# One queue for all first inputs of a two-layer adaLN, FFN and expert kernel, in a new order, and ones from a set tile

## The chip, the cores and the metric

The kernel runs on one core of one Trainium2 chip. The metric is the device time in microseconds of one execution, as the median over runs. The core has five engines that run their own instruction lists: TensorE (PE, with its weight loads shown apart as PEld), VectorE (DVE), ScalarE (ACT), GpSimd (POOL) and SyncE (SP). Transfers between memory and the on-chip buffer are issued from SP's queue and ScalarE's queue (and GpSimd's, for indirect ones) and are carried by 16 DMA engines. Engines wait for each other and for transfers on semaphores.

## The reference

The input x is 32 x 32 x 512 numbers; each of the two layers adds the output of a feed-forward block to x, and each block works on a conditioned version of x.

```python
# layer 0
c0 = conv1d(x, L0_cond_weight, groups=4, taps=9, pad=4) + (cond @ c_weight.T)[:, :, None] + bias
g, u = octonion_linear(c0, ternary(w_gate)), octonion_linear(c0, ternary(w_up))   # 512 -> 1360
x = x + octonion_linear(silu(g) * u, ternary(w_down))                            # 1360 -> 512
# layer 1
h = gelu(cond @ W0 + b0); h = gelu(h @ W1 + b1); att = softmax(h @ W2 + b2)       # 32 x 8
y = mix of 8 channel kernels by att, applied to x, plus att @ bias_k
out = x + top-2-of-32 experts of y (512 x 512 each, routed per token)
```

`ternary(W)` is scale * clip(round(W / scale), -1, 1) with scale = mean(|W|) over the whole table, so nothing of a table can be quantized before all of it has been read and summed.

## The kernel before

All is written by hand as one instruction list per engine, with semaphores; the order of each list is the order of the code. What matters here is the start, the first 16 of 280 us. The small arrays lie in host-packed groups: `nets` (condition, the small nets' weights, biases, a row of constants) is one array of 281 KB, `cf` (identity matrix, counters, masks, a block of ones) one of 187.5 KB, `mix` holds the sign patterns `perm` in its first half.

The steps of the start, by engine, with lines of the kernel before:

- SP (L566 to L580) issues without waiting: `base[0]` (gate table, 352 KB), `perm` (256 KB), `wc` (taps, 192 KB), `xp_first` (half of the padded input, 1040 KB), `base[1]` and `base[2]` (up and down tables), `sel`, the rest of `mix`, `xp_second`, `kept`, `eb`, `x` into `acc`, and two fills of memory tables.
- ScalarE (L753, L754) issues `nets` and `cf` as its first two instructions.
- VectorE sets `fill` and `unit` (L919, L920, a 128 x 128 tile of ones), then for table m: `magnitudes(m)` (L926, sum of |base|), `scales(m)` (L931 to L933), `quantize_first(m)` (L940, L941).
- TensorE: ten `fills` (L1398, matmuls on a constant tile whose result nobody reads), `scale(0)` (L1348: ones times the row sums), two fills, the first net layer (L1407), the context (L1409 and L1410, where `ones` times a row adds the bias), fills and second net layer, `gate_table(0)` and `(1)` (L1357), the convolution's first block (L1330), the third net layer (L1421, L1422, again with `ones`), two gate tables, `scale(1)`, the second block, two gate tables, the third block, two gate tables, and `across_conv` (L1340, transposes by the identity matrix in `cf`).

`pe.wait_ge(cf_in, 16)` stands ahead of the first net layer. VectorE waits for `cf` only after the down table's scale (after L1008), and the ternary remainder on GpSimd (L670 to L673) follows `thr_done`.

Of the kernel before, what the change touches and what calls it, by code (L numbers as in the profile page):

```python
# [42 lines left out]
P = 128  # L43
NB, CH, D = 32, 32, 512
# [13 lines left out]
KC = 8  # L58
# [160 lines left out]
def split(ap, group):  # L219

    out, at = [], 0
    for _, w in GROUPS[group]:
        out.append(ap[:, at:at + w])
        at += w
    return out


def build_adaln_ffn(nc, a):
    ctx = ExitStack()
    with ctx:  # L230
# [21 lines left out]
        def put(name, shape, dt, at):  # L252
            return nc.alloc_sbuf_tensor_at(name, shape, dt, offset=at)

        def own(name, shape, dt):
            n = 4 if dt != BF16 else 2
            for s in shape[1:]:
                n *= s
            return put(name, shape, dt, region(n))
# [41 lines left out]
        nets = su.put("nets", [P, NETS], F32)  # L301
# [3 lines left out]
        cond, cwt, w0s, w1s, w2s, b01, rows = split(nets[:], "nets")  # L305
# [3 lines left out]
        base = put("base", [P, 3, BW], F32, r_h + 2 * HC * HALF * 4 - 3 * BW * 4)  # L309
# [3 lines left out]
        unit = put("unit", [P, P], F32, r_t + 2 * D * 4 + 1024)  # L313
# [45 lines left out]
        cf = own("cf", [P, CF_W], F32)  # L359
# [39 lines left out]
        NETS_BANK, SCALE_BANK = bank[4], bank[7]  # L399
# [25 lines left out]
        def sem(name):  # L425
            return ctx.enter_context(nc.semaphore(name))

        wc_in, cf_in, nets_in, mix_in, sel_in, kept_in, eb_in = (
            sem(s) for s in ("wc_in", "cf_in", "nets_in", "mix_in", "sel_in", "kept_in", "eb_in"))
        base_in = [sem(f"base_in{m}") for m in range(3)]  # L430
# [7 lines left out]
        ctx_mm = sem("ctx_mm")  # L438
        h1_mm, h1_done, h2_mm, h2_done = (sem(s) for s in ("h1_mm", "h1_done", "h2_mm", "h2_done"))
        att_mm, att_out, att_max, att_exp, att_done = (sem(s) for s in ("att_mm", "att_out", "att_max", "att_exp", "att_done"))  # L440
# [52 lines left out]
        ones = cf[:, C_ONE:C_ONE + P]  # L493

        def rec_parts(g):

            tiles, parts_ = GROUPS_OF_TILES[g], []
            for q, (p0, w, _, pos) in enumerate(tiles[0]):
                ranks = [tile[q][2] for tile in tiles]
                runs = [0] + [i for i in range(1, len(ranks)) if ranks[i] != ranks[i - 1] + 1] + [len(ranks)]  # L500
                for i0, i1 in itertools.pairwise(runs):
                    same = [p for p in parts_ if [p[0] + p[1], p[2], p[3] + p[1], p[4:]] == [p0, ranks[i0], pos, [i0, i1]]]
                    if same:
                        same[0][1] += w
                    else:
                        parts_.append([p0, w, ranks[i0], pos, i0, i1])
            return parts_
# [9 lines left out]
        def height(t):  # L517

            return sum(w for _, w, _, _ in TILES[t])
# [44 lines left out]
        def _(sp):  # L564

            sp.dma_start(base[:, 0], a["base"][:, 0]).then_inc(base_in[0], 16)  # L566
            sp.dma_start(mix[:, 0:OCT * P // 2], a["mix"][:, 0:OCT * P // 2]).then_inc(perm_in, 16)
            sp.dma_start(wc[:], a["wc"]).then_inc(wc_in, 16)
            sp.dma_start(xp_first[:], a["xp"][:, 0:NB // 2]).then_inc(xp_in[0], 16)
            for m in range(1, 3):  # L570
                sp.dma_start(base[:, m], a["base"][:, m]).then_inc(base_in[m], 16)
            sp.dma_start(sel[:], a["sel"]).then_inc(sel_in, 16)
            sp.dma_start(mix[:, OCT * P // 2:], a["mix"][:, OCT * P // 2:]).then_inc(mix_in, 16)
            sp.dma_start(xp_second[:], a["xp"][:, NB // 2:]).then_inc(xp_in[1], 16)
# [175 lines left out]
        @block.scalar  # L750
        def _(act):

            act.dma_start(nets[:], a["nets"]).then_inc(nets_in, 16)  # L753
            act.dma_start(cf[:], a["cf"]).then_inc(cf_in, 16)  # L754

            def conv_hi(i):
                act.wait_ge(across_mm, i + 1)
# [563 lines left out]
        def _(pe):  # L1321
            mm = nc.tensor.matmul
# [13 lines left out]
            def across_conv(i):  # L1336

                pe.wait_ge(convs_done, i + 1)
                for b in range(NPT):
                    v = nc.tensor.transpose(ACROSS[FIRST_TILES[i]][:, P * b:P * (b + 1)], convs[:, i % 2, b], ident)  # L1340
                v.then_inc(across_mm, 1)
# [8 lines left out]
            def gate_table(k):  # L1350

                if k == 0:
                    pe.wait_ge(tern_done, 1)
                    pe.wait_ge(perm_in, 16)
                if k >= 2:
                    pe.wait_ge(pg_done, k - 1)
                mm(in_bank(PG[k % 2], 0, CUT), perm[:, k], chunks(0, CUT)(tern[:, 0]), start=True, stop=True).then_inc(pg_mm, 1)  # L1357

            def up_table(k):

                if k == 0:
                    pe.wait_ge(tern_done, 2)
                if k >= 2:
                    pe.wait_ge((pu_even, pu_odd)[k % 2], k // 2)
                mm(in_bank(PU[k % 2], 0, CUT), perm[:, k], chunks(0, CUT)(tern[:, 1]), start=True, stop=True).then_inc(pu_mm, 1)
# [29 lines left out]
            def fills(count):  # L1395

                for _ in range(count):
                    mm(bank[0][:], fill[:, 0:P], fill[:], start=True, stop=True)  # L1398
# [4 lines left out]
            scale(0)  # L1403
            fills(2)
            pe.wait_ge(nets_in, 16)
            pe.wait_ge(cf_in, 16)
            mm(NETS_BANK[:, 0:NB], w0s, cond, start=True, stop=True).then_inc(h1_mm, 1)  # L1407
            pe.wait_ge(thr_done, 1)
            mm(SCALE_BANK[:, 0:NB], cwt, cond, start=True, stop=False)  # L1409
            mm(SCALE_BANK[:, 0:NB], rows[0:1, 0:P], ones[0:1, 0:NB], start=False, stop=True).then_inc(ctx_mm, 1)  # L1410
            fills(1)
            pe.wait_ge(h1_done, 1)
            mm(NETS_BANK[:, NB:2 * NB], w1s, h1[:], start=True, stop=True).then_inc(h2_mm, 1)
# [5 lines left out]
            conv(0, (0,))  # L1419
            pe.wait_ge(h2_done, 1)  # L1420
            mm(NETS_BANK[0:NB, 64:64 + KC], h2[:], w2s, start=True, stop=False)  # L1421
            mm(NETS_BANK[0:NB, 64:64 + KC], ones[0:1, 0:NB], rows[0:1, P:P + KC], start=False, stop=True).then_inc(att_mm, 1)  # L1422
            gate_table(2)
            gate_table(3)
            scale(1)
# [4 lines left out]
            gate_table(6)  # L1430
            gate_table(7)
            pe.wait_ge(att_out, 1)
            across_conv(0)
            up_table(0)
            pe.wait_ge(thr_done, 2)
# [167 lines left out]
            def product(t, c0, c1):  # L1603

                if c0 == 0:
                    pe.wait_ge(xt_done, t + 1)
                    if t >= 2:
                        pe.wait_ge(res_done, t - 1)
                    if t < 2:
                        pe.wait_ge(h_done, 2 * HC)  # L1610
                    for _, _, r, _ in TILES[t]:
                        pe.wait_ge(w_in[buffer(r)], loads_of(r))
                for c in range(c0, c1):
                    for p0, w, r, _ in TILES[t]:
                        v = mm(RS[t % 2][p0:p0 + w], xT[x_slot(t)][:, c, p0:p0 + w], wbuf[buffer(r)][:, c], start=(c == 0), stop=(c == DC - 1))  # L1615
                if c1 == DC:
                    v.then_inc(r_mm, 1)
# [269 lines left out]
```

## Time and profile before

| | us |
|---|---|
| median of 3 runs | 280.45 (280.31 to 280.61) |
| profiled execution | 282.07 |
| its span | 280.2 |
| TensorE busy | 263.7 (94%) |
| VectorE busy | 143.0 (51%) |
| ScalarE busy | 77.8 (28%) |
| GpSimd busy | 68.8 (25%) |

The span runs from the first to the last recorded instruction; the execution's own time is 1.9 us longer. The shares are means over the whole span. In the first 1/40 of it TensorE's digit is 7 and DMA's 7, then DMA stands at 9 for four slices, so the start is a stretch of its own. "Idle before" in a row names what ended the wait. A landing time is the time from a transfer's issue to the semaphore that tells it is complete.

### The profile page before, as it was taken

Reading aid. Unit: us, or ns where it says so; the run is one execution under the profiler, and the core shown is the slowest. Engines: PE = TensorE matmul, PEld = TensorE weight load, DVE = VectorE, ACT = ScalarE, POOL = GpSimd, SP = SyncE. Lnnn points to the kernel's source line nnn. Section 1 sums busy time; section 2 is a strip of 40 time slices with the busy share of each in tenths; the row PEclk is TensorE's granted clock in tenths of the full one; section 3 lists DMA queues with packets and bytes.
Section 4 is the critical chain, followed back from the end, with each engine's and each line's share of the span. In section 5 each row is a group of like instructions: output and inputs, shape, how many; then the busy total and the mean of one; then the engine's idle time right before and its main releaser. Section 6 shows DMA issues by size and latency. Waiting matters only on the chain.

```text
span 280.2 us, 4479 instructions
## 1 busy us (share of the span) xinstructions
PE 263.7 (94%) x1584; PEld 157.3 (56%) x1584; DVE 143.0 (51%) x420; ACT 77.8 (28%) x144; POOL 68.8 (25%) x67
## 2 busy tenths in 40 slices
PE   7988999999999999999999999999979999998970
PEld 2456676688866678878886664423333433332750
DVE  2677765766913341577441445510558521440695
ACT  1665564334221215223321222221010101113100
POOL 0621600000000000004605023445755352133200
PEclk9999999999999999999999999999999999999996
DMA  7999900000000100019807999944899999994945
GB/s 256 399 374 328 291 18 1 2 0 2 0 37 37 40 1 37 2 25 388 338 2 251 394 425 422 418 146 113 326 321 388 414 420 421 423 378 168 413 163 223
DMA packets 19590, 61.69 MB, mean 220 GB/s; under 512 B 4698, under 2 KB 6394, under 8 KB 15216
## 3 DMA queue, kind: packets, MB, share of 16 engines
q1 hardware_dynamic: 14816, 51.03, 47.6%
q0 software_dynamic: 3312, 7.80, 7.5%
q10 hardware_dynamic: 1440, 2.58, 2.5%
q8 instruction: 13, 0.21, 0.3%
q14 instruction: 9, 0.07, 0.1%
HBM read 54.39 MB, written 13.21 MB: 241 GB/s over the span
## 4 chain that ended last, share of the span: by engine, by line
PE 75%; DVE 10%; DMA 8%; issue 2%; another core or an unknown queue 2%; SPq 1%; ACT 1%; DVEq 0%; ACTq 0%; POOLq 0%
PE bank L1447 28%; PE bank L1615 16%; PE bank L1650 15%; PE bank L1502 3%; DMA xp_first<-in_xp 3%; DVE acc L1303 3%; DMA wbuf<-r_tab 3%; PE bank L1588 2%; PE bank L1330 2%; DMA r_tab<-res,recs 2%; PE bank L1509 1%; DVE acc L1077 1%; PE bank L1340 1%; DVE xT L1109 1%
## 5 line engine op out<-in xcount | busy, mean ns | idle before, releaser
L1615 PE MATMUL bank<-wbuf,xT 128*32 128x512 f32 (+1 forms) x448 | 70.5, 598 | 1.6 <-DVE xT L1109 0.9
L1650 PE MATMUL bank<-md,hid 128*128 128x512 f32 x176 | 49.6, 418 | 0.0
L683 POOL DMA_INDIRECT slots<-kept,sid x16 | 15.9, 996 | 120.3 <-DVE sid L1072 117.3
L1615 PEld LDWEIGHTS bank<-wbuf,xT 128*32 128x32 f32 (+1 forms) x448 | 18.7, 119 | 37.7 <-issue 34.6
L1650 PEld LDWEIGHTS bank<-md,hid 128*128 128x128 f32 x176 | 31.3, 189 | 8.9 <-issue 4.1
L1447 PE MATMUL bank<-y0hi,mg 128*128 128x512 f32 x88 | 35.2, 412 | 0.2 <-ACT y0hi L758 0.2
L1447 PE MATMUL bank<-y0hi,mu 128*128 128x512 f32 x88 | 33.7, 396 | 0.7 <-DVE mu L958 0.7
L1447 PE MATMUL bank<-y0lo,mu 128*128 128x512 f32 x88 | 33.6, 393 | 0.0
L1447 PE MATMUL bank<-y0lo,mg 128*128 128x512 f32 x88 | 33.5, 392 | 0.0
L1109 DVE COPY xT<-bank 128x512 f32<-128x512 f32 x19 | 12.9, 690 | 38.5 <-PE bank L1588 32.7
L880 ACT ACTIVATE res<-bank,recs 128x512 f32<-128x512 f32 x19 | 13.1, 688 | 67.8 <-PE bank L1615 52.4
L1018 DVE TENSOR_TENSOR htmp<-bank,stmp 128x512 f32<-128x512 f32 x22 | 15.2, 690 | 28.9 <-PE bank L1447 18.4
L690 POOL DMA_INDIRECT yg<-y_tab,recs x19 | 19.4, 1021 | 18.3 <-DMA recs<-slots 13.1
L698 POOL DMA_INDIRECT r_tab<-res,recs x16 | 17.0, 1064 | 26.6 <-ACT res L880 21.9
L803 ACT ACTIVATE hid<-htmp 128x512 fp32r<-128x512 f32 x22 | 13.9, 630 | 24.4 <-DVE htmp L1018 22.4
L799 ACT ACTIVATE stmp<-bank,small 128x512 f32<-128x512 f32 x22 | 15.2, 689 | 17.9 <-PE bank L1447 17.6
L1028 DVE SCALAR_TENSOR_TENSOR acc<-bank,small,acc 128x512 f32<-128x512 f32 x8 | 6.0, 750 | 25.8 <-PE bank L1650 19.8
L1447 PEld LDWEIGHTS bank<-y0hi,mg 128*128 128x128 f32 x88 | 16.5, 188 | 4.7 <-issue 1.5
L1447 PEld LDWEIGHTS bank<-y0hi,mu 128*128 128x128 f32 x88 | 16.5, 188 | 4.7 <-ACT mu L773 1.1
L1447 PEld LDWEIGHTS bank<-y0lo,mg 128*128 128x128 f32 x88 | 16.5, 188 | 3.3 <-issue 0.2
L1447 PEld LDWEIGHTS bank<-y0lo,mu 128*128 128x128 f32 x88 | 16.4, 188 | 3.2
L1022 DVE TENSOR_TENSOR hid<-htmp,hid 128x512 fp32r<-128x512 f32 x22 | 16.0, 729 | 0.9 <-ACT hid L803 0.3
(205 smaller groups left out, 289.9 us busy)
## 6 DMA issues: line engine op xcount, KB each, us to landing
wbuf<-in_w SPq DMA_DIRECT2D x32, 1024.0 KB, 12.8
r_tab<-in_zero SPq DMA_DIRECT2D x1, 4096.0 KB, 24.7
wbuf<-r_tab SPq DMA_DIRECT2D x8, 512.0 KB, 7.7
acc<-in_x SPq DMA_DIRECT2D x1, 2048.0 KB, 14.6
y_tab<-yv SPq DMA_DIRECT2D x8, 256.0 KB
out<-acc ACTq DMA_DIRECT2D x8, 256.0 KB, 2.3
base<-in_base SPq DMA_DIRECT2D x3, 352.0 KB, 7.6
xp_first<-in_xp SPq DMA_DIRECT2D x1, 1040.0 KB, 7.5
```

Of the source, the lines that this page charges most:

```text
L683: pool.indirect_dma_start(out=slots, out_offset=bass.IndirectOffsetOnAxis(ap=sid[:, j, k:k + 1], axis=0), in_=rec[:, j, k], in_offset=None ...
L690: pool.indirect_dma_start(out=yg[b][0:rows_], out_offset=None, in_=y_tab[0:HALF] if first else y_tab, in_offset=bass.IndirectOffsetOnAxis( ...
L698: pool.indirect_dma_start(out=r_tab, out_offset=bass.IndirectOffsetOnAxis(ap=recs[0:rows_, slot, 1:2].bitcast(U32), axis=0), in_=res[b][0: ...
L799: nc.scalar.activation(stmp[:, n % 2], G[n % 2][:], ACT.Silu, scale=wsc[:, 0:1]).then_inc(silu_done, 1)
L803: nc.scalar.activation(hid[:, :, 0, n % HC], tiles_of(htmp[:, n % 2]), ACT.Copy).then_inc(hhi_done, 1)
L880: nc.scalar.activation(res[b][0:rows_], bank_[0:rows_], ACT.Copy, scale=recs[0:rows_, slot, 2:3].bitcast(F32)).then_inc(res_done, 1)
L1018: nc.vector.tensor_tensor(htmp[:, n % 2], UU[n % 2][:], stmp[:, n % 2], ALU.mult).then_inc(h_done, 1)
L1022: nc.vector.tensor_tensor(hid[:, :, 1, n % HC], tiles_of(htmp[:, n % 2]), hid[:, :, 0, n % HC].bitcast(F32), ALU.subtract).then_inc(hlo_do ...
L1109: nc.vector.tensor_copy(xT[half_][:].rearrange("p c t -> p (c t)"), bank_[:]).then_inc(xt_done, 1)
L1447: v = mm(bank_[:], tab[:, r, n % HC], (y0hi, y0lo)[part][half][:, r], start=(r == 0 and part == 0), stop=(r == R - 1 and part == 1))
L1615: v = mm(RS[t % 2][p0:p0 + w], xT[x_slot(t)][:, c, p0:p0 + w], wbuf[buffer(r)][:, c], start=(c == 0), stop=(c == DC - 1))
L1650: v = mm(DN[j % 2][:], hid[:, t, part, c], md[:, c], start=(c == 0 and part == 0), stop=(c == HC - 1 and part == 1))
```

## The change

`nets` and `cf` are issued by SP's queue and no longer by ScalarE's. On SP's queue `nets` stands second, after `base[0]`; `cf` stands between `base[1]` and `base[2]`. The two small matrix products that multiply by a row of ones read it from the tile `unit` that VectorE sets, in place of the block of ones in `cf`. TensorE's wait for `cf` moves from the first net layer to the first transposes.

```diff
             sp.dma_start(base[:, 0], a["base"][:, 0]).then_inc(base_in[0], 16)
+            sp.dma_start(nets[:], a["nets"]).then_inc(nets_in, 16)
             sp.dma_start(mix[:, 0:OCT * P // 2], a["mix"][:, 0:OCT * P // 2]).then_inc(perm_in, 16)
             sp.dma_start(wc[:], a["wc"]).then_inc(wc_in, 16)
             sp.dma_start(xp_first[:], a["xp"][:, 0:NB // 2]).then_inc(xp_in[0], 16)
-            for m in range(1, 3):
-                sp.dma_start(base[:, m], a["base"][:, m]).then_inc(base_in[m], 16)
+            sp.dma_start(base[:, 1], a["base"][:, 1]).then_inc(base_in[1], 16)
+            sp.dma_start(cf[:], a["cf"]).then_inc(cf_in, 16)
+            sp.dma_start(base[:, 2], a["base"][:, 2]).then_inc(base_in[2], 16)
...
-            act.dma_start(nets[:], a["nets"]).then_inc(nets_in, 16)
-            act.dma_start(cf[:], a["cf"]).then_inc(cf_in, 16)
...
             pe.wait_ge(nets_in, 16)
-            pe.wait_ge(cf_in, 16)
             mm(NETS_BANK[:, 0:NB], w0s, cond, start=True, stop=True).then_inc(h1_mm, 1)
...
-            mm(SCALE_BANK[:, 0:NB], rows[0:1, 0:P], ones[0:1, 0:NB], start=False, stop=True).then_inc(ctx_mm, 1)
+            mm(SCALE_BANK[:, 0:NB], rows[0:1, 0:P], unit[0:1, 0:NB], start=False, stop=True).then_inc(ctx_mm, 1)
...
-            mm(NETS_BANK[0:NB, 64:64 + KC], ones[0:1, 0:NB], rows[0:1, P:P + KC], start=False, stop=True).then_inc(att_mm, 1)
+            mm(NETS_BANK[0:NB, 64:64 + KC], unit[0:1, 0:NB], rows[0:1, P:P + KC], start=False, stop=True).then_inc(att_mm, 1)
...
             pe.wait_ge(att_out, 1)
+            pe.wait_ge(cf_in, 16)
             across_conv(0)
```

SP's queue at the start of the program, before:

```order
L566 DMA base<-in_base 128x704
L567 DMA mix<-in_mix 128x512
L568 DMA wc<-in_wc 128x384
L569 DMA xp_first<-in_xp 128x2080
L571 DMA base<-in_base 128x704 x2
L572 DMA sel<-in_sel 32x192
```

And after:

```order
L566 DMA base<-in_base 128x704
L567 DMA nets<-in_nets 128x562
L568 DMA mix<-in_mix 128x512
L569 DMA wc<-in_wc 128x384
L570 DMA xp_first<-in_xp 128x2080
L571 DMA base<-in_base 128x704
L572 DMA cf<-in_cf 128x375
L573 DMA base<-in_base 128x704
L574 DMA sel<-in_sel 32x192
```

`nets` and `cf` are two more rows on this queue, and every transfer from `perm` on is issued one place later, from `base[2]` on two. On ScalarE the same two rows are gone:

```order
-L750 UNCONDITIONAL_BRANCH [waits barrier_Pool_Activation_PE_DVE_SP_release]
-L753 DMA nets<-in_nets 128x562
-L754 DMA cf<-in_cf 128x375
+L752 UNCONDITIONAL_BRANCH [waits barrier_Pool_Activation_PE_DVE_SP_release]
 L762 ACT_TABLE_LOAD
 L762 ACTIVATE h_67<-bank,nets 128x32 [waits h1_mm]
```

ScalarE's first own work is now the table load. On TensorE no instruction changes its place; at the net layers and the transposes the waits and operands change:

```order
-L1407 MATMUL bank<-nets 128x32 [waits cf_in,nets_in]
-L1409 MATMUL bank<-nets 128x32 [waits thr_done]
-L1410 MATMUL bank<-cf,nets 128x32
+L1406 MATMUL bank<-nets 128x32 [waits nets_in]
+L1408 MATMUL bank<-nets 128x32 [waits thr_done]
+L1409 MATMUL bank<-unit,nets 128x32
```

The wait for `cf` is now part of the first transpose's row, L1340, ahead of all transposes.

## Rows read from the trace of the kernel before

**Rows 1.** Chain of waits, first 40 us: start us, us, what

```profile
2.09 7.51 DMA xp_first<-in_xp
...
11.92 1.07 PE bank L1330 x32
```

**Rows 2.** Timeline, TensorE: start, us, engine line operation [idle before]

```profile
1.43 4.45 PE L1398 MATMUL bank<-fill 128*128 128x512 bf16 x10 [1.43 <-DVE fill L919]
...
6.45 0.35 PE L1348 MATMUL bank<-asum,unit 128*128 128x1 f32 x2 [0.58 <-DVE mag L926]
...
7.70 0.40 PE L1410 MATMUL bank<-cf,nets 1*128 1x32 f32 x2
...
8.62 0.49 PE L1357 MATMUL bank<-tern,mix 128*128 128x384 bf16 x2
...
9.74 1.15 PE L1330 MATMUL bank<-xp_first,wc 32*32 32x512 f32 x32 [0.63 <-DMA xp_first<-in_xp]
...
11.54 0.38 PE L1348 MATMUL bank<-asum,unit 128*128 128x1 f32 x2
...
15.52 0.63 PE L1340 MATMUL bank<-cf,convs 128*128 128x128 f32 x4 [0.59 <-DVE convs L948]
```

**Rows 3.** Timeline, VectorE

```profile
5.41 0.89 DVE L926 SCALAR_TENSOR_TENSOR mag<-base 128x704 f32<-128x704 f32 x1 [3.89 <-DMA base<-in_base]
...
8.44 0.18 DVE L982 COPY cbt<-bank 128x32 f32<-128x32 f32 x1
10.58 0.89 DVE L926 SCALAR_TENSOR_TENSOR mag<-base 128x704 f32<-128x704 f32 x1 [1.97 <-issue]
11.40 0.08 DVE L926 DVE_READ_ACCUMULATOR mag<-base 128x1 f32 x1
```

**Rows 4.** Timeline, SP's and ScalarE's queues

```profile
0.70 0.40 SPq L566 DMA_DIRECT2D base<-in_base  x1
...
1.15 0.46 ACTq L754 DMA_DIRECT2D cf<-in_cf  x1
...
2.90 1.20 SPq L571 DMA_DIRECT2D base<-in_base  x2
```

**Rows 5.** Transfers by source: KB each, median us to landing; last, the three of base

```profile
base<-in_base SPq DMA_DIRECT2D x3, 352.0 KB, 7.6
...
nets<-in_nets ACTq DMA_DIRECT2D x1, 281.0 KB, 4.8
...
cf<-in_cf ACTq DMA_DIRECT2D x1, 187.5 KB, 5.5
...
DMA to landing us min/median/max: 4.7/7.6/7.8
```

**Rows 6.** Stretches: bounds, length, busy time of each engine, PEclk, DMA share, GB/s

```profile
2.20:3.70 1.50, 1.50 (x5) 0.60 (x4) 0.00 (x0) 0.72 (x1) 0.00 (x0) 1.00 0.76 236
...
2.20:8.00 5.80, 5.22 (x19) 2.37 (x17) 1.94 (x7) 1.00 (x2) 0.59 (x1) 1.00 0.99 377
2.20:8.55 6.35, 5.77 (x23) 2.78 (x21) 2.49 (x8) 1.00 (x2) 1.14 (x1) 1.00 0.98 374
2.20:8.95 6.75, 6.17 (x25) 2.93 (x23) 2.56 (x8) 1.29 (x3) 1.54 (x2) 1.00 0.98 375
2.20:9.45 7.25, 6.33 (x25) 2.93 (x23) 2.56 (x8) 1.76 (x5) 2.04 (x2) 1.00 0.98 375
4.40:8.60 4.20, 3.62 (x18) 2.05 (x17) 2.54 (x8) 0.29 (x1) 1.19 (x1) 1.00 1.05 419
9.60:15.00 5.40, 5.19 (x108) 1.65 (x108) 3.04 (x10) 4.01 (x11) 3.33 (x5) 1.00 1.03 395
37.00:45.00 8.00, 8.00 (x40) 5.68 (x40) 4.37 (x9) 3.91 (x8) 0.00 (x0) 1.00 0.00 0
```

**Rows 7.** Timeline, ScalarE

```profile
7.44 0.29 ACT L762 ACTIVATE h<-bank,nets 128x32 f32<-128x32 f32 x1 [4.52 <-PE bank L1407]
...
9.87 1.28 ACT L783 ACT_TABLE_LOAD   x1
```

## The prediction

> **What bounds the kernel now.** I read the table of busy shares first, then the chain of waits of the first 40 us, then the rows of TensorE, VectorE and the queues in the first 16 us, the landing times, and last the stretches with their DMA rates. TensorE is busy for 94% of the span. The change touches only the first 16 us, so the questions are what TensorE waits for there, and whether time won there reaches the end.
>
> In the chain of the first 40 us the longest piece is a transfer: xp_first, issued at 2.09 and landed 7.51 us later, at 9.60 [rows 1]. The convolution's first block starts right behind it, at 9.74. TensorE was ready before: its two gate tables run from 8.62 to 9.11, and then it is idle for 0.63 us with that transfer named as the releaser [rows 2]. What held it before the tables is a chain from the first weight table: base[0] lands at 0.70 + 4.7 = 5.40 [rows 4, 5], VectorE's pass over it starts at 5.41 and takes 0.89 us [rows 3], and the scale product follows at 6.45, after 0.58 us of idle TensorE [rows 2].
>
> There is a second gate of the same kind. The scale of the second table runs on TensorE at 11.54 [rows 2], just behind the close of VectorE's pass over base[1] at 11.40 + 0.08. That pass starts at 10.58, though VectorE was free from 8.62 on [rows 3], and base[1] was issued at 2.90 and lands 7.6 later, at 10.5 [rows 4, 5]. So two landings, xp_first and base[1], set the first and the second block of the convolution. The constants cf, in contrast, land at 1.15 + 5.5 = 6.65 [rows 4, 5], while their first large use is the transposes at 15.52 [rows 2].
>
> **The transfers as a tally of bytes.** Ahead of the end of xp_first stand base[0] 352, nets 281 and cf 187.5 KB [rows 5], and perm 256, wc 192 and xp_first itself 1040 KB by the shapes of the issues (128 x 512, 128 x 384 and 128 x 2080 numbers of four bytes): 2308.5 KB, which is 2364 thousand bytes. From 2.20 to 8.55 us the core moves 374 GB/s x 6.35 us = 2375 thousand [rows 6]. So the sum is passed at about 8.5, and xp_first lands at 9.6: the slowest of the 16 engines is some 1.05 us behind the mean. base[1] shows the same: 2724 thousand bytes, passed at 9.45 (375 x 7.25 = 2719) [rows 6], landed at 10.5. Landings follow the bytes queued ahead, so this tally serves for the new order.
>
> **The change, part by part.**
> cf behind base[1]: 187.5 KB, 192 thousand bytes, go from ahead of both gates to behind them. At the rate of that stretch, 419 GB/s [rows 6], this is 0.46 us. By the tally, xp_first's 2172 thousand bytes are passed just before 8.00 (377 x 5.80 = 2187), so it lands at 9.05, 0.55 earlier; base[1]'s 2532 thousand at 8.95 (375 x 6.75 = 2531) [rows 6], so it lands at 10.0, 0.50 earlier. The bounds are 0.46 and 0.55; I take 0.50, that of base[1], since its gate is the later one.
>
> nets behind base[0]: 281 KB are ahead of xp_first either way. But base[0] now has the DMA engines alone: its 360 thousand bytes are passed at 3.7 (236 x 1.50 = 354) [rows 6], plus 1.0 is 4.7 in place of 5.4, and VectorE is done with it at 5.6. TensorE's ten fills run until 1.43 + 4.45 = 5.88 [rows 2] and become the gate: the scale product starts at 5.9 in place of 6.45, 0.55 earlier. nets has base[0] and itself ahead, what the two queues had moved when base[0] landed before, so it comes at 5.4 to 5.5; its product is due at 6.5, behind the scale and two fills. All up to the gate tables moves by 0.55, and TensorE is free at 8.56. xp_first comes at 9.05, so TensorE still stands for about 0.6 us, and this part gives nothing by itself. Were its cover gone it would be worth up to 0.55.
>
> The first block then starts at 9.24, the second scale at 11.04, the second block at 11.42 in place of 11.92 [rows 1]. Next in line is ScalarE: its table load at 9.87 [rows 7] follows the copies of the first gate tables and moves by 0.55 with them, so it is not late.
>
> cf itself has the 2724 thousand bytes ahead that base[1] had, and lands at about 10.5. Its new wait stands in front of the first transposes, due at 15.0 (15.52 less 0.5). All of TensorE's later work would stand behind it, but there are 4.5 us to spare. base[2] and all later transfers have the same bytes ahead as now.
>
> `unit` in place of `ones` costs nothing: same shape and form, one such product taking 0.40 us in two passes [rows 2], and `unit` is read by the scale product before.
>
> ScalarE loses two issues, 0.46 us for the second [rows 4], and nothing gains by it, as it is idle for 4.52 us before its first activation [rows 7]. SP issues two transfers more, some 0.45 us each. xp_first is issued at 2.55 in place of 2.09, and the 1081 KB ahead of it keep the engines busy until past 5 us, so it is still in time.
>
> The Trainium skill (DMA: Bandwidth & Descriptors, Issuing engines are not separate DMA queues) states that starting transfers from several engines saves only the sequencer's time to start them. Read against this change, what is given up is one issue ahead of xp_first; if its landing hung on its issue, the sum would be 0.05 in place of 0.50 us. This trace disagrees with that reading: xp_first needs 7.51 us to land while its own 1065 thousand bytes take 2.5 us at 419 GB/s.
>
> **Does it reach the end?** From 16 us on the engines hand work to each other. Between 37 and 45 us the core moves 0 GB/s [rows 6]: the queued inputs are all in, and every transfer behind them starts on something computed. So the 0.50 should arrive whole: profiled execution 282.07 - 0.50 = 281.57 (span 279.7). The median of the runs, 280.45, stands 1.62 below the profiled time; with the same difference it becomes 279.95. 0.2% is 0.56 us, about what a measurement of this kernel can tell from no change. The forecast is a small gain just inside it.
>
> **The rivals.**
> Rival A, the gain is lost again (0 to 0.15 us, time 280.4). For: the 1.05 us by which the slowest engine trails is known only as a size, and may grow where base[0] alone meets the first, slow packets (236 GB/s before 3.7 us against 419 later [rows 6]). A wait late in the kernel could also swallow 0.5 us. Against: both gates show the same 1.05. Chance 0.21.
>
> Rival B, both gates open earlier than the bytes say (gain up to 1.1, time 279.35). TensorE is free at 8.56; with xp_first landed by then, the first block starts 1.1 us earlier, and base[1] would have to be there at 9.4. For: two queues that take turns may cost the engines something that one doesn't. Against: from 4.4 us on the rate is already as high as anywhere, so it would have to be won in the first 2 us. Chance 0.16.
>
> Rival C, slower: one queue moves only its own share. The rate of one queue alone in the first 2 us is not shown. If SP's queue moves no more there than it did beside the other, then the 288 thousand bytes of nets come on top, 288 / 419 = 0.69 us, and the absence of cf gives nothing. xp_first lands at 10.3, the first block starts at 10.43, time 281.15. It decides once SP's queue alone stays at half of the full rate between 2.2 and 5.4 us. Against: from 9.6 to 15.0 us SP's queue is the only one and moves 395 GB/s [rows 6]. Chance 0.09.
>
> Rival D, that the change doesn't do what it says, is closed: the order of SP's queue has nets second and cf behind base[1].
>
> **How the numbers follow.** Forecast 0.54, A 0.21, B 0.16, C 0.09. The forecast's own range is 279.6 to 280.3 (gain 0.15 to 0.85). Its middle is 0.06 short of the bound of 0.2% at 279.89, so 0.45 of it counts as faster. Faster: 0.54 x 0.45 + 0.16 = 0.40. Slower: 0.09. Same: 0.51. The range is 279.3 to 280.8: it takes in A and B, and reaches halfway to C.
>
> **What would show it.** In the changed kernel's profile VectorE's pass over base[0] starts at 4.7, the scale product at 5.9, and the gate tables end near 8.6. TensorE still stands about 0.6 us for xp_first, the first block starts at 9.24, VectorE's pass over base[1] at 10.1, the second block at 11.4. The transposes at 15.0 don't wait for cf. All later events stand 0.5 earlier, and the span is 0.5 shorter. The forecast is wrong if xp_first lands after 9.4 or before 8.7, if a row before 16 us waits for cf or nets, or if the 0.5 is there at 16 us and gone at 120.

## The result, and the profile after

The changed kernel takes 281.00 us (median of 20 runs, 280.21 to 282.02), and before runs beside it at 280.07 (20 runs, 279.72 to 282.51). The ratio is 1.003, with a 95% interval of 1.0016 to 1.0043. That is 0.84 us slower (the medians themselves differ by 0.93), where I had forecast 0.50 faster. The time lies outside my range.

The profiled execution of the changed kernel took 280.79 us (span 279.0), near its median. The one of before that the prediction was made from took 282.07 us (span 280.2), 1.6 to 2 us above its medians. For the late part of the kernel I therefore use a second profile of before, called `b4_before` below (280.59 us, span 278.7, its median 280.09). From 10 to 178 us the two profiles of before agree within 0.05 us nearly everywhere; the first falls 2.05 us behind between 178 and 211 us. Line numbers shift by one or two between the two kernels.

**The front.** Chain of waits of the changed kernel, first 40 us, to stand beside [rows 1]:

```profile
2.58 6.61 DMA xp_first<-in_xp
...
9.32 1.15 PE bank L1330 x32
...
11.50 1.07 PE bank L1330 x32
```

Timeline of the changed kernel, TensorE, as [rows 2]:

```profile
1.43 3.92 PE L1398 MATMUL bank<-fill 128*128 128x512 bf16 x10 [1.43 <-DVE fill L919]
5.19 0.28 PE L1348 MATMUL bank<-asum,unit 128*128 128x1 f32 x2
...
7.28 0.49 PE L1357 MATMUL bank<-tern,mix 128*128 128x384 bf16 x2
9.32 1.15 PE L1330 MATMUL bank<-xp_first,wc 32*32 32x512 f32 x32 [1.55 <-DMA xp_first<-in_xp]
...
11.12 0.38 PE L1348 MATMUL bank<-asum,unit 128*128 128x1 f32 x2
...
15.10 0.63 PE L1340 MATMUL bank<-cf,convs 128*128 128x128 f32 x4 [0.59 <-DVE convs L948]
```

Its timeline, VectorE, as [rows 3]:

```profile
3.97 0.89 DVE L926 SCALAR_TENSOR_TENSOR mag<-base 128x704 f32<-128x704 f32 x1 [2.46 <-DMA base<-in_base]
...
10.16 0.89 DVE L926 SCALAR_TENSOR_TENSOR mag<-base 128x704 f32<-128x704 f32 x1 [2.89 <-issue]
```

SP's queue in the changed kernel, as [rows 4]:

```profile
0.71 0.40 SPq L566 DMA_DIRECT2D base<-in_base  x1
...
2.58 0.43 SPq L570 DMA_DIRECT2D xp_first<-in_xp  x1
...
3.52 0.51 SPq L572 DMA_DIRECT2D cf<-in_cf  x1
```

Transfers of the changed kernel by source, as [rows 5]; the last line is that of base's three:

```profile
xp_first<-in_xp SPq DMA_DIRECT2D x1, 1040.0 KB, 6.6
...
nets<-in_nets SPq DMA_DIRECT2D x1, 281.0 KB, 3.8
...
cf<-in_cf SPq DMA_DIRECT2D x1, 187.5 KB, 7.1
...
DMA to landing us min/median/max: 3.2/7.0/7.6
```

Stretches of the changed kernel, as [rows 6] (the last number is GB/s), and ScalarE's first activation and its table load, as [rows 7]:

```profile
2.20:3.70 1.50, 1.50 (x5) 0.60 (x4) 0.00 (x0) 0.00 (x0) 0.00 (x0) 1.00 0.92 314
4.40:8.60 4.20, 3.37 (x20) 2.19 (x18) 2.13 (x8) 1.52 (x5) 2.44 (x3) 1.00 1.00 358
```

```profile
6.10 0.29 ACT L762 ACTIVATE h<-bank,nets 128x32 f32<-128x32 f32 x1 [4.10 <-PE bank L1406]
...
8.53 1.28 ACT L783 ACT_TABLE_LOAD   x1
```

The gates moved as intended. base[0] lands at 3.9 instead of 5.4, VectorE's second pass starts at 10.16 instead of 10.58, and the first block starts at 9.32 instead of 9.74. TensorE now reaches that block much too soon. Its tables end at 7.77, so it stands for 1.55 us, where it stood for 0.63 [rows 2]. The rate between 4.4 and 8.6 us is 358 GB/s in place of 419 [rows 6]. But the second block is 0.42 earlier (11.50 against 11.92), so in this trace the front doesn't hold the loss.

**The end.** I followed the shift between the changed kernel and `b4_before` through both traces: the changed kernel is 0.34 to 0.39 us ahead from 26 us until 242 us, within the GpSimd stores of the results. Timelines, GpSimd, the last three stores. First `b4_before`, then the changed kernel:

```profile
238.74 0.98 POOL L698 DMA_INDIRECT r_tab<-res,recs  x1 [3.11 <-ACT res L880]
243.22 1.80 POOL L698 DMA_INDIRECT r_tab<-res,recs  x1 [3.49 <-ACT res L880]
247.07 0.98 POOL L698 DMA_INDIRECT r_tab<-res,recs  x1 [2.06 <-ACT res L880]
```

```profile
238.37 0.98 POOL L700 DMA_INDIRECT r_tab<-res,recs  x1 [3.11 <-ACT res L880]
242.54 0.98 POOL L700 DMA_INDIRECT r_tab<-res,recs  x1 [3.19 <-ACT res L880]
246.99 1.82 POOL L700 DMA_INDIRECT r_tab<-res,recs  x1 [3.46 <-ACT res L880]
```

Each kernel has one store that takes 1.8 us instead of 0.98. It is the last but one in before and the last in the changed kernel. In before, GpSimd then waits for 2.06 us instead of 3.2, so the slow store costs nothing. In the changed kernel SP's read of the results waits for it. The ScalarE evacuation that feeds the slow store (the copy of a finished product out of its bank) is late too. Chains of waits from 245 us on, `b4_before` and the changed kernel:

```profile
245.51 0.04 ACTq L879
245.55 0.05 issue
245.59 0.70 ACT res L880
...
247.07 6.80 DMA r_tab<-res,recs
253.87 0.02 issue
253.89 0.03 SPq L658
```

```profile
245.13 0.04 ACTq L879
245.17 0.34 issue
245.51 0.70 ACT res L880
...
246.99 7.54 DMA r_tab<-res,recs
254.54 0.02 issue
254.55 0.03 SPq L660
```

ScalarE has what it waits for at 245.17 in the changed kernel, 0.38 ahead of before, but stands for 0.34 us as "issue" where before stands for 0.05. The lead is down to 0.08 when the store starts. The store lands 7.54 instead of 6.80 us later, and SP reads back 0.66 us later than before.

The bill from this pair of traces is about 0.3 us on ScalarE plus 0.74 on GpSimd's store, 1.04 in all, less 0.38 won at the front: 0.66 at 254.5 us. The spans differ by only 0.3 (279.0 against 278.7), because the read-back behind the store was slow in `b4_before`. Chains, the read-back's last part, `b4_before` and the changed kernel:

```profile
256.49 9.08 DMA wbuf<-r_tab
```

```profile
256.94 8.85 DMA wbuf<-r_tab
```

From the store's landing to the addition on VectorE that waits for this transfer (265.69 and 265.92) it is 11.8 us in `b4_before` and 11.4 in the changed kernel. That gives 0.4 us back, and no more than chance is needed for it: before's own three traces differ by 0.6 us there. This much was read, not shown. The experiments had to tell this reading from the others.

### The profile page after: what moved, and what is told of

It is laid out like the page before. It is cut to its first block, busy times and chain, and to the rows that moved or that the text cites. A ratio compares the mean times of both kernels' runs of the same rounds, so it can differ in the third digit from the quotient of the medians.

```text
span 279.0 us, 4478 instructions
## 1 busy us (share of the span) xinstructions
PE 262.7 (94%) x1584; PEld 157.5 (56%) x1584; DVE 142.9 (51%) x420; ACT 77.9 (28%) x144; POOL 68.8 (25%) x67
## 4 chain that ended last, share of the span: by engine, by line
PE 79%; DMA 8%; DVE 7%; issue 2%; SPq 1%; ACT 1%; DVEq 0%; ACTq 0%; POOLq 0%
PE bank L1447 29%; PE bank L1615 18%; PE bank L1650 15%; DMA wbuf<-r_tab 3%; PE bank L1502 3%; PE bank L1588 3%; DMA r_tab<-res,recs 3%; PE bank L1330 2%; DMA xp_first<-in_xp 2%; DVE acc L1303 2%; PE bank L1509 1%; PE bank L1340 1%; DVE acc L1308 1%; PE bank L1392 1%; PE bank L1559 1%
```

## The experiments

A ratio is that of the kernel's time to that of before, run beside it on the same chip. Each group of experiments ran on one chip, the four groups on four. On the chips of the first and fourth group the times scatter more (before took 283.7 and 283.3 us there), so their intervals are wide.

**First group: which part of the change.** `a4_before_again` is before, `a1_after_again` the changed kernel. The two others each put one of the two transfers on SP and leave the other on ScalarE:

```diff
 a2_nets_only (against before)
             sp.dma_start(base[:, 0], a["base"][:, 0]).then_inc(base_in[0], 16)
+            sp.dma_start(nets[:], a["nets"]).then_inc(nets_in, 16)
...
-            act.dma_start(nets[:], a["nets"]).then_inc(nets_in, 16)
 a3_cf_only (against the changed kernel)
-            sp.dma_start(nets[:], a["nets"]).then_inc(nets_in, 16)
...
+            act.dma_start(nets[:], a["nets"]).then_inc(nets_in, 16)
```

> The kernel before, unchanged, for a second profile of it and as a measure of noise. Ratio 1.000 within 0.2%. The first profile of it has a span of 280.2 us, while its median of 280.07 stands for a span of about 278.3. If the extra 1.9 us of that profile is a late event (two waits of 1.83 and 2.94 us for gathered rows at 200.9 and 203.5 us), this profile has a span near 278.3 and those waits are short. If it lies at the start, the first block of the convolution starts at another time than 9.74.

> The changed kernel again. Theory S (the time won at the start is real and lost late): first block of the convolution near 9.3, ratio 1.003. Theory N (the measured loss was chance): ratio 0.998 to 1.000.

> The kernel before with one edit: nets second on SP's queue; cf stays on ScalarE's queue, still with its wait at the first net layer and its block of ones. By the tally of bytes xp_first lands as before, so no gain at 16 us (within 0.1 us). Theory Q (nets on SP's queue is what costs later): ratio 1.003 or more. Theory T (the earlier start of the compute is what costs later): ratio 1.000, since nothing starts earlier.

> The changed kernel with nets back on ScalarE's queue: cf alone moves behind base[1], with the ones from the set tile. By the tally the whole gain of 0.4 to 0.5 us at 16 us is here. Theory T (earlier start costs later): ratio 1.003. Theory Q (the queue of nets costs): ratio 0.998 to 0.999.

Measured: a4 0.9982 (0.9945 to 1.0018), a1 1.0028 (0.9975 to 1.008), a2 1.0021 (0.9985 to 1.0058), a3 0.9991 (0.9943 to 1.0039). No interval excludes no change, so the times decide nothing. The front did not come as expected: xp_first landed at 9.81 in a2 and at 9.36 in a3, beside 9.43 in a4, so a3 gained 0.07 us where 0.4 to 0.5 was expected, and in a1 it landed at 10.11. a4's span is 281.0 on this chip, not 278.3, so it did not tell where the first profile's excess lies; `b4_before` did. The traces showed two things more. In a2 and a3 no store is slow at all. In a1 TensorE waited even longer for xp_first, and its clock fell. Timeline and stretches of a1, TensorE (in a stretch the third number from the end is the granted clock):

```profile
10.25 1.15 PE L1330 MATMUL bank<-xp_first,wc 32*32 32x512 f32 x32 [2.46 <-DMA xp_first<-in_xp]
```

```profile
8.00:10.00 2.00, 0.00 (x0) 0.00 (x0) 0.00 (x0) 1.97 (x4) 1.21 (x2) 1.00 1.01 356
...
11.60:14.90 3.30, 3.30 (x40) 1.12 (x39) 2.22 (x9) 1.30 (x5) 1.59 (x2) 0.50 0.99 381
```

After 2.46 us of idle TensorE the clock stood at 0.50, its 1.2 GHz level, from 11.60 to 14.90. From the first block's start to VectorE's first pass over the convolution's results (L948) it took 6.25 us, in the changed kernel 4.94. That is 1.3 us. It gave a rival: the clock (theory K) instead of a loss at the end of the kernel.

**Second group: the wait ahead of the first block, and the time of arrival.**

```diff
 b1_filled (against the changed kernel: five fill matmuls cover the idle time)
+            fills(5)
             pe.wait_ge(wc_in, 16)
 b2_late (two behind xp_first's wait: all starts later)
+            fills(2)
             conv(0, (0,))
```

`b3_after` is the changed kernel and `b4_before` before.

> The changed kernel with five more idle-time matmuls (0.22 us each at the full clock, about 1.1 us) between the two gate tables and the wait for the taps and xp_first. They fill most of TensorE's idle time there and end before xp_first lands. Theory K: the clock doesn't fall in any execution, and the ratio to the kernel before is 0.998 to 0.999. Theory L: no change against the changed kernel, ratio 1.003.

> The changed kernel with two matmuls on the constant tile behind the wait for xp_first, so that the convolution starts 0.43 us later, as in the kernel before, while the queues are those of the changed kernel. If an earlier start is what the late stage dislikes (theory T), the ratio is 1.000. If the queue or the instruction list is (theory Q), the time is that of the changed kernel plus 0.4 us: ratio 1.004 to 1.005.

> The changed kernel once more. Theory K (the clock): TensorE idle for 1.5 to 2.5 us ahead of the first block; where xp_first lands past 10 us the granted clock falls to half for 3.4 us from about 11.5 and the first blocks end 1.3 us later, ratio 1.003 to 1.006; where it lands near 9.2 the clock stays and this stage ends 0.4 earlier than in the kernel before. Theory L (a loss in the late stage between 180 and 260 us, whatever the start): ratio 1.003 with the clock whole.

> The kernel before once more, for a profile beside one of the changed kernel from the same chip. Ratio 1.000 within 0.2%. TensorE idle for 0.5 to 0.7 us ahead of the convolution's first block, no fall of the granted clock before 270 us.

Measured: b1 1.0044 (1.0031 to 1.0057), b2 1.0044 (1.0031 to 1.0057), b3 1.0054 (1.002 to 1.0087), b4 0.9994 (0.9974 to 1.0014). In b1's trace the clock doesn't fall in the front, and its first block starts at 9.68 with no idle time ahead of it. It is still 1.2 us slower than before. So a clock that falls in the front is not the main loss. The clock fell elsewhere, which I had not expected: near 257 us in b1, b2 and b4, beside 2.78, 3.47 and 1.99 us of idle TensorE. b4 is before itself, and its chain of waits doesn't run through TensorE there. b2 speaks against the reading that stores slow down by the hour at which they come: its last store starts at 247.59, 0.5 us later than that of `b4_before`, and is as slow (it lands 7.80 us after its start, b1's 7.71). The first profile of before has its slow store at 245.27 and a last one of 0.98 us at 249.12. b3 repeats the changed kernel's result and, like a1, its clock fell, after only 1.19 us of idle time. Its timeline and stretch:

```profile
9.91 1.74 PE L1330 MATMUL bank<-xp_first,wc 32*32 32x512 f32 x32 [1.19 <-DMA xp_first<-in_xp]
```

```profile
10.50:11.50 1.00, 1.00 (x32) 0.00 (x0) 0.75 (x1) 0.47 (x2) 0.00 (x0) 0.50 1.09 421
```

Then I counted. In each trace I numbered ScalarE's recorded instructions. In before there are 218, in the changed kernel 216: the two DMA issues are gone. a2 and a3 have 217. The 0.34 us stand between the 191st record and the 192nd whenever there are 218 or 216. The 192nd is an evacuation both times, but two places further down the program in the changed kernel. With 217 the 192nd record is a wait that ends 3.4 us after ScalarE's last work, and no such delay shows; that the wait hides one is a guess. This is a theory with a sharp test: add one instruction at the head of ScalarE's list, change nothing else, and the slow store must vanish. Add two and it must go back to its place in before. A rival is closed by the traces at hand: GpSimd's longer wait alone doesn't slow a store. The slow stores come behind waits of 3.46 and 3.49 us, but in a3 two others come behind 3.38 and 3.93 us and take 1.03.

**Third group: the length of the list alone.**

```diff
 c1_one_more (against the changed kernel; c2_two_more has the line twice)
         @block.scalar
         def _(act):
+            act.sem_inc(pool_steps, 1)
 c3_short_list (against before: cf and nets on SP ahead of both gates)
             sp.dma_start(base[:, 0], a["base"][:, 0]).then_inc(base_in[0], 16)
+            sp.dma_start(nets[:], a["nets"]).then_inc(nets_in, 16)
+            sp.dma_start(cf[:], a["cf"]).then_inc(cf_in, 16)
...
-            act.dma_start(nets[:], a["nets"]).then_inc(nets_in, 16)
-            act.dma_start(cf[:], a["cf"]).then_inc(cf_in, 16)
...
+            fills(5)
             pe.wait_ge(wc_in, 16)
 c4_filled_one (against the changed kernel: b1's fills and c1's line)
```

> The changed kernel with one more instruction at the head of ScalarE's list (an increment of a semaphore that nobody waits for). In all ten traces so far ScalarE stands for 0.34 us at one place of its own list, and in all eight whose list is two shorter or as long as before, the store of a result tile behind it takes 1.80 us on GpSimd in place of 0.98. Theory P (the place in ScalarE's list, counted in instructions, is what costs): with one more instruction that place falls between two tiles, no late store takes 1.80 us, and the ratio to the kernel before is 0.998 to 0.999. Theory D (something else in the moved transfers costs): ratio 1.003 to 1.005 as without it.

> The changed kernel with two such instructions, so that ScalarE's list is as long as in the kernel before. Theory P: the 1.80 us fall on the last but one store of all, which hides them, as in the kernel before; ratio 0.998 to 0.999. Theory D: ratio 1.003 to 1.005.

> The kernel before with nets and cf second and third on SP's queue, so that the bytes ahead of xp_first are those of the kernel before and ScalarE's list is two shorter; its wait for cf and its block of ones stay; five more matmuls on the constant tile ahead of the convolution fill TensorE's wait. No gain at 16 us (convolution's first block within 0.15 of 9.7). Theory P: the last store takes 1.80 us, ratio 1.003 to 1.005. Theory D, with cf's new place or unit as the cause: ratio 1.000.

> The changed kernel with both edits: five more matmuls on the constant tile ahead of the wait for xp_first (so that the clock can't fall there) and one more instruction in ScalarE's list. Theory P: ratio 0.998 to 0.999 and the narrowest spread of all; Theory D: 1.003.

Measured: c1 1.0021 (0.9995 to 1.0046), c2 1.0019 (0.9995 to 1.0042), c3 1.003 (1.0011 to 1.005), c4 0.9999 (0.999 to 1.0008). Timelines, GpSimd, the last two stores of c1, of c2 and of c3:

```profile
242.25 0.98 POOL L700 DMA_INDIRECT r_tab<-res,recs  x1 [3.19 <-ACT res L881]
246.40 0.98 POOL L700 DMA_INDIRECT r_tab<-res,recs  x1 [3.17 <-ACT res L881]
```

```profile
242.86 1.80 POOL L700 DMA_INDIRECT r_tab<-res,recs  x1 [3.49 <-ACT res L882]
246.71 0.98 POOL L700 DMA_INDIRECT r_tab<-res,recs  x1 [2.06 <-ACT res L882]
```

```profile
243.70 0.98 POOL L700 DMA_INDIRECT r_tab<-res,recs  x1 [3.19 <-ACT res L880]
248.15 1.82 POOL L700 DMA_INDIRECT r_tab<-res,recs  x1 [3.46 <-ACT res L880]
```

With one instruction more no store is slow, and the last one lands 6.71 us after its start, not 7.54. With two the slow store is back in before's place. c3 has the bytes ahead of both gates that before has, but the short list, and its last store is slow. The place of the slow store is thus set by the length of ScalarE's list and by nothing else that I changed. It was where this says in all 17 traces, on several chips. Profiled spans: c1 277.9, c2 278.0, against 279.0 for the changed kernel and 278.7 for `b4_before`.

The trace of c2 gives the price with the front held equal. It runs within 0.05 us of the changed kernel's from the first block until 242 us, and its last store stands as follows in the chain of waits:

```profile
246.71 6.77 DMA r_tab<-res,recs
```

It lands at 253.48, the changed kernel's at 254.54, and the spans are 1.0 us apart. Two idle instructions took 1.06 us away.

The times of c1 and c2 missed my numbers. The four slowest executions of c1 (281.37 to 284.06 us) have granted clocks of 0.979 to 0.984 and the eight others 0.988 and more; of c2's three slowest, two have 0.984 and 0.976, the slowest (282.79) has 0.988. Both kernels keep the bare idle time ahead of the first block, so the clock probably falls there in some of their executions; I have no trace of a slow one. c4, which also covers the idle time, has no such tail (279.34 to 280.61). It can't be told from before (I had expected 0.998 to 0.999), and its interval lies wholly below the changed kernel's. It differs from b1 by one idle instruction alone, and b1 stood at 1.0044 (1.0031 to 1.0057), on another chip: about 1.3 us. c4 is the best version I found, but it is not shown to beat before.

c3 spoke to rival C too. Stretches from 4.4 to 8.6 us of `b4_before` and of c3, which have the same bytes ahead of the first block on two queues and on one:

```profile
4.40:8.60 4.20, 3.33 (x20) 2.08 (x18) 2.56 (x8) 0.58 (x2) 1.56 (x2) 1.00 1.03 402
```

```profile
4.40:8.60 4.20, 4.20 (x23) 2.79 (x22) 2.01 (x8) 1.11 (x4) 2.11 (x2) 1.00 1.01 354
```

With one queue the first block starts at 10.52, with two at 9.72, where I had expected 9.7 for both. But this trace of c3 is of an execution of 282.29 us, 1.05 above c3's median, so it is one of c3's slower executions.

**Fourth group: repeats, and one queue against two.** `d1_cf_only` is a3, `d2_filled_again` is c4, and `d3_one_queue` is c3 with c1's extra line, so that its list has the harmless length.

> cf alone moved behind base[1] and ones from the set tile; nets on ScalarE's queue as before, so ScalarE's list is one shorter and its costly place falls between tiles. Theory R (two queues move more than one at the start): rate from 4.4 to 8.6 us near 400 GB/s, first block at 9.2 to 9.4, ratio 0.998. Rival (the rate is chance): ratio equal to that of the next kernel within 0.1%.

> The changed kernel with five more matmuls ahead of the wait for xp_first and one more instruction in ScalarE's list, again. Theory R: rate from 4.4 to 8.6 us 350 to 390 GB/s, first block 9.2 to 9.9, ratio 0.999 to 1.000, above that of the kernel that moves cf alone. Rival: 0.998 to 0.999.

> nets and cf second and third on SP's queue, ahead of xp_first as in the kernel before by bytes, with five more matmuls ahead of the convolution and one more instruction in ScalarE's list, so that no late store is slow. The tally of bytes says: first block at 9.7, ratio 1.000. Theory R: xp_first lands 0.5 to 0.9 us later than with two queues, first block at 10.2 to 10.6, ratio 1.002 to 1.003.

Measured: d1 1.0002 (0.996 to 1.0044), d2 0.9976 (0.9933 to 1.0019), d3 1.0033 (1.0 to 1.0067). None has a slow store, as the length of 217 asks. Theory R of these expectations, that two queues move more than one, is not borne out. d1 has two queues and moved 385 GB/s between 4.4 and 8.6 us, and its first block started at 9.69, not at 9.2 to 9.4. d2, with one queue, moved 398 and started it at 9.14. d3, with one queue and before's bytes, moved 387. Its first block starts at 9.90, but not because of xp_first, which was issued at 3.05 and landed at 9.33, earlier than in any trace of before. Its five fills ran that long. Timeline of d3, TensorE:

```profile
8.72 1.24 PE L1399 MATMUL bank<-fill 128*128 128x512 bf16 x5
9.90 1.14 PE L1331 MATMUL bank<-xp_first,wc 32*32 32x512 f32 x32
```

d3's ratio fits theory R, but its interval reaches the 1.000 of the tally too. On this chip the times settle no more than that d2 is not slower than before by over 0.2%.

## Why the prediction was wrong

**The step that failed: "ScalarE loses two issues ... and nothing gains by it", and with it "So the 0.50 should arrive whole".** I priced the two removed instructions by the engine's idle time at their own place. Their removal also moves every later instruction two places up its list, and at one place of this list the engine stands 0.34 us. That delay lay over the last but one evacuation, where GpSimd's wait of some 3 us for the last one covered it. It came to lie over the last one, where nothing does. Price: 0.3 us on ScalarE and 0.7 to 0.8 on the store behind it. c1, c2 and c3 show that the length of the list moves it; b1 against c4 and the trace of c2 show the price. Why ScalarE stands there at all is open.

The first half of the argument held. In the result's trace the shift of the front did arrive whole, 0.39 us at 26 us and 0.38 still at 242 us. Rival A came nearest in kind: it let something late swallow the gain, but not more than the gain. I had asked whether some wait swallows it, and never whether the engine's own list has costly places. No row of the first 16 us could have told. The traces of before do show a 1.8 us store among 0.98 us ones, and I had not looked at the end of the kernel at all.

**The term that was mis-sized: 0.50 for cf behind base[1].** It rested on the tally at an unchanged 419 GB/s. In the result's trace it was nearly right (xp_first landed at 9.19, forecast 9.05), but over all traces it was not. Landings of xp_first, issue plus time to landing, in us:

```
two queues, before's order (before, a4, b4): 9.43 9.59 9.60; mean 9.54
two queues, cf alone behind base[1] (a3, d1): 9.36 9.55; mean 9.46
one queue, changed order (changed, a1, b1 to b3, c1, c2, c4, d2): 8.77 8.89 9.02 9.13 9.19 9.48 9.51 9.77 10.11; mean 9.32
one queue, before's bytes (c3, d3): 9.33 10.39; mean 9.86
```

The gain is 0.22 on the mean, and the scatter within the changed order is six times as large. Part of that is the chip: on the two chips that have both orders, the changed one was later by 0.68 (a1 against a4) or within 0.2 of before (b1, b2 and b3 against b4). So these traces don't show a gain of the front beyond the result's pair. The rate from 4.4 to 8.6 us was 402 to 419 GB/s in before's order, 372 and 385 with cf alone moved and still two queues, and 347 to 411 with one queue. The lower rate thus doesn't go with the number of queues, and its cause is open. Rival C, slower by one queue's share, did not happen: the changed kernel moved more at first (314 GB/s from 2.2 to 3.7, before 236 [rows 6]), and its xp_first landed at 9.19, not at 10.3.

The Trainium skill (DMA: Bandwidth & Descriptors, Issuing engines are not separate DMA queues) says that issuing from several engines only saves sequencer time. By it xp_first should land in c3 and d3 as in before, since its issue, at 3.05, is still far ahead of its turn. It landed 0.85 us later than before's mean in c3 and 0.21 earlier in d3, so these runs don't decide against the page.

**The idle time of TensorE, forecast at 0.6.** base[0] came at 3.9, not 4.7, because it moved faster at first (314 GB/s, above). The ten fills ended at 5.35, as the last two took 0.38 us each where before's took some 0.63, and the tables ended at 7.77 instead of 8.56. In b1, b2, b3 and c1 all ten fills were as long as before's, and the tables ended at 8.36 to 8.72, as forecast. The wait was 0.66 to 2.46 us over the six traces of this order that have no fills ahead of it (the changed kernel, a1, b2, b3, c1, c2). I had written that this part "gives nothing by itself". In fact it can cost: in a1 and b3 the clock fell to 1.2 GHz, at a price of 1.3 us. The Trainium skill (TensorE: Matmul & The Clock Gate, Part 1: The HAM clock gate) says that the gate releases by recent activity and closes again after idle time. The two falls came behind idle time, and none came in the front of the four traces in which fills left none (b1, c4, d2, d3). Why the four other waits of 0.66 to 1.55 us passed without one, these runs don't tell. In the changed kernel's 20 executions of the result the granted clock was 0.988 to 0.993 throughout, so there it explains nothing. It probably explains most of the tails of c1 and c2.

**What was right.** cf landed at 3.52 + 7.1 = 10.6 (forecast 10.5), and the transposes at 15.10 (forecast 15.0) waited for VectorE and not for cf. VectorE's second pass came at 10.16 (10.1), the first block at 9.32 (9.24), the second at 11.50 (11.42), in this one trace. `unit` for `ones` took the same 0.40 us.

The sum now: 0.22 won at the front on the mean, 1.06 lost at the end, makes 0.84 slower. Measured: 0.84. That the two agree so well is luck: the first term scatters by more than its size.

## What to carry to other kernels

Removing or adding an instruction moves all later ones along that engine's list, and a list can have a place at which the engine stands. Before believing a small result, look for the one instruction of a repeated group that is slower than its fellows, see where it lies before and after, and test it with one idle instruction at the head of the list. Moving an input earlier than its consumer can use it only turned into idle time elsewhere here, and on TensorE that can cost the clock. Fills in the same edit cover it, but they too can end later than the input lands (d3). One trace of each order is not enough to size a change in when transfers land: take several, of both orders on one chip.

## What the runs showed of the hardware

- ScalarE stood 0.34 us (0.340 to 0.344) ahead of its 192nd recorded instruction in the ten traces with 216 or 218 records, and the GpSimd indirect store fed by it took 1.80 to 1.82 us instead of 0.98. As the last store it landed 7.27 to 7.80 us after its start in five traces, where a last store of 0.98 us took 6.64 to 6.89 in seven; the other traces with a last store on the chain of waits, a1 with a slow one (5.09) and a3, d1 and d2 (4.22 to 5.14), lie lower. Neither the hour nor the chip mattered, only the place in the list. Why the engine stands there, and why GpSimd's own instruction grows with it, is open. Other lengths were not tried, nor a change of another engine's list by itself.
- In the front TensorE's clock fell to 0.5 near 1.19 us (b3) and 2.46 us (a1) of idle time and stayed up around 1.55 (changed kernel), 1.33 (c2), 1.25 (c3), 1.22 (b2) and 1.01 (a2). The length of the wait alone does not say whether it falls. Late in the kernel it fell beside waits of 1.99 (b4), 2.78 (b1), 3.47 (b2), 4.36 (d2) and 4.88 us (d1), and not beside 1.99 (changed kernel), 2.26 (a1), 2.32 (a4), 2.58 (a3) and 2.59 (d3).
- xp_first landed at 8.77 to 10.11 us over nine traces of the same transfer order.
